# A conditioned linear layer and a mixture of experts in float32: a reordered first block, moved low parts, and a woven seam between the shared part and the experts

## The reference, cut to what matters

```python
ys = y / sqrt(512)                                        # conditioned linear layer
d  = rsqrt(einsum('bi,io->bo', ys*ys, weight*weight) + 1e-8)
x  = x + einsum('bsi,io->bso', x * ys[:, None, :], weight) * d[:, None, :]

shared = silu(x @ w1) * (x @ w3) @ w2                     # hidden size 1024
s      = sigmoid(concat([x, t_emb]) @ router_W)           # 8 experts
pick 2 of 8 by s + router_bias, gates = s / sum of the two
routed = sum over the two experts of gate * (gelu(x @ W1e) @ W2e)   # hidden size 512
x = x + (shared + routed) / 3
```

## Time and profile before

| | us |
|---|---|
| median of 3 runs (lowest, highest) | 1060.47 (1059.27, 1061.65) |
| the profiled execution | 1054.4 |
| its span, first to last instruction | 1052.6 |
| PE busy | 1021.2 (97%) |
| DVE, ACT, POOL busy | 506.2, 293.0, 331.5 |

### The profile page before, as it was taken

One profiled execution on the slowest core, in us unless ns is written; L12 is line 12 of the kernel. 1 busy time (PEld: TensorE's weight loads), 2 busy tenths in 40 slices (PEclk: granted clock), 3 DMA queues, 4 the chain that ended last, 5 costly groups with the idle time before them and its releaser, 6 DMA issues.

```text
span 1052.6 us, 14602 instructions
## 1 busy us (share of the span) xinstructions
PE 1021.2 (97%) x4692; PEld 836.1 (79%) x4692; DVE 506.2 (48%) x828; ACT 293.0 (28%) x461; POOL 331.5 (31%) x393
## 2 busy tenths in 40 slices
PE   6999999999999999999999998999999999999996
PEld 5888778887888888888888886788888888878874
DVE  4555456668333333333322214555655566555653
ACT  3222252332222222122211112333333233332331
POOL 2000000001214433334312401365554645545533
PEclk9999999999999999999999999999999999999999
DMA  4666688787876677876833576999778999999984
GB/s 172 200 206 217 222 281 255 259 318 248 294 239 233 221 267 253 264 268 212 290 100 90 190 202 205 239 221 231 147 147 179 226 221 231 210 215 226 228 180 80
DMA packets 133259, 228.61 MB, mean 217 GB/s; under 512 B 29041, under 2 KB 83953, under 8 KB 125105
## 3 DMA queue, kind: packets, MB, share of 16 engines
q1 hardware_dynamic: 60400, 144.06, 42.8%
q0 software_dynamic: 31328, 64.11, 26.4%
q10 hardware_dynamic: 41472, 19.68, 7.9%
HBM read 112.85 MB, written 98.38 MB: 201 GB/s over the span
## 4 chain that ended last, share of the span: by engine, by line
PE 83%; DMA 8%; DVE 4%; SPq 2%; issue 2%; ACT 1%; POOLq 0%; DVEq 0%
PE banks L530 13%; PE banks L532 12%; PE banks L531 12%; PE banks L468 8%; PE banks L469 8%; PE banks L470 8%; DMA we_d<-ehl 5%; PE banks L482 4%; PE banks L483 4%; PE banks L484 4%; PE banks L416 3%; PE banks L417 3%; PE banks L418 3%; DMA eraw<-expert_w 2%; SPq L286 1%
## 5 line engine op out<-in xcount | busy, mean ns | idle before, releaser
L468 PE MATMUL banks<-xh,w 128*128 128x512 f32 x512 | 199.6, 390 | 1.8 <-DVE xl L725 1.8
L469 PE MATMUL banks<-xl,w 128*128 128x512 f32 x512 | 199.2, 389 | 0.0
L470 PE MATMUL banks<-xh,w 128*128 128x512 f32 x512 | 199.2, 389 | 0.0
L1184 POOL DMA_INDIRECT out<-ys,slot x71 | 124.0, 1746 | 181.1 <-DVE ys L1080 89.4
L792 DVE SCALAR_TENSOR_TENSOR gm<-sil,banks 128x512 f32<-128x512 f32 x64 | 43.9, 685 | 240.7 <-ACT sil L611 234.6
L1073 DVE TENSOR_TENSOR hidtl<-hidt,hidth 128x512 fp32r<-128x512 f32 x71 | 49.1, 692 | 165.9 <-ACT hidth L685 165.2
L611 ACT ACTIVATE sil<-banks 128x512 f32<-128x512 f32 x64 | 38.2, 597 | 291.9 <-PE banks L470 291.9
L1170 POOL DMA_DIRECT2D xg<-xs_d x136 | 99.9, 1108 | 58.8 <-DVE xgt L1054 49.6
L530 PE MATMUL banks<-we,hidth 128*128 x284 | 112.2, 395 | 5.8 <-issue 5.5
L530 PE MATMUL banks<-we,xgth 128*128 x284 | 111.1, 391 | 3.4 <-issue 3.4
L468 PEld LDWEIGHTS banks<-xh,w 128*128 128x128 f32 x512 | 96.1, 188 | 22.3 <-issue 2.3
(11 more groups left out here) (163 smaller groups left out, 1512.0 us busy)
## 6 DMA issues: line engine op xcount, KB each, us to landing
we_d<-ehl SPq DMA_DIRECT2D x32, 1024.0 KB, 7.3
we<-we_d SPq DMA_DIRECT2D x48, 512.0 KB
hturn<-hid ACTq DMA_DIRECT2D x284, 64.0 KB
xg<-xs_d POOLq DMA_DIRECT2D x136, 128.0 KB
eraw<-expert_w SPq DMA_DIRECT2D x32, 512.0 KB
x1t_d<-x1t SPq DMA_DIRECT2D x8, 1024.0 KB, 8.8
xin<-x1t_d SPq DMA_DIRECT2D x8, 1024.0 KB, 8.8
x_d<-x1tok SPq DMA_DIRECT2D x32, 256.0 KB
```

What stands on the lines that cost most here:

```text
L468: pe.matmul(ps[hc % 2][:, :], w_hi, xh[:, j, c, :], start=(c == 0), stop=False)
L469: pe.matmul(ps[hc % 2][:, :], w_hi, xl[:, j, c, :], start=False, stop=False)
L470: last = pe.matmul(ps[hc % 2][:, :], w_lo, xh[:, j, c, :], start=False, stop=(c == DC - 1))
L1184: pool.indirect_dma_start(out[:, :], IO(slot[:, t, 0:1], 0), ys[:, t % RING, :], None, compute_op=ALU.add).then_inc(added[t % 2], 16)
```

## The change

1. The condition's DMA goes from the head of SP's queue to the head of POOL's; the squares `w0sq` go from POOL to DVE, behind the low parts of block 0 and ahead of those of block 1.
2. `first_linear` waits for each kind of product by itself: four matmuls high x high once `wmh` and `xh` are there, four with `wml`, four with `xl`.
3. At the end of part one `x_low` runs once behind each `x1t`.
4. In block 0 of part two the first weight piece's cast and low part go from step 0 to step 1.
5. In the last block of part two `matmul1(0)` goes in between `down(7, 6)` and `down(7, 7)`, the table is read ahead of `up(7, 7)`, and DVE's and ACT's first steps of part three go into or right behind step 6 and 7 of block 7, with `take_x(1)`, `take_x(2)`, `turn_x(2)`, `turn_x(3)` ahead of `output(7)`. `hturn` and `hidth` change places in memory, so that only `h_high_of(0)` waits for `output(7)`.
6. In every tile of part three ACT's cast `x_high_of` is that of tile `t+2` and stands between `hidden(t)` and `move_h(t)`; it waits for DVE's `turn_x(t+2)`. DVE's order stays as it was for tiles 2 to 68.
7. At the end PE does `matmul1(70)` ahead of `matmul2(66)`, ACT moves tile 70 behind `h_high_of(68)`, and DVE's `take_y` goes behind `take_h`.

```diff
-        hturn = sb("hturn", [RING, SUB, P], FP32, 160)
+        hturn = sb("hturn", [RING, SUB, P], FP32, 128)
-        hidth = sb("hidth", [2, DC, P], FP32R, 132)
+        hidth = sb("hidth", [2, DC, P], FP32R, 160)
...
-            sp.dma_start(cnd[:, :, :], condT).then_inc(cond_in, 16)
...
                 for c in range(DC):
+                    pe.wait_ge(wmh_ready, c + 1)
+                    pe.wait_ge(xh_ready, c + 1)
+                    for o in range(DC):
+                        pe.matmul(lin_ps[o][:, :], wmh[:, 0, c, o * P:(o + 1) * P], xh[:, 0, c, :], start=(c == 0), stop=False)
                     pe.wait_ge(wml_ready, c + 1)
+                    for o in range(DC):
+                        pe.matmul(lin_ps[o][:, :], wml[:, 0, c, o * P:(o + 1) * P], xh[:, 0, c, :], start=False, stop=False)
                     pe.wait_ge(xl_ready, c + 1)
                     for o in range(DC):
-                        last = part(0, o, c, 0)
+                        last = pe.matmul(lin_ps[o][:, :], wmh[:, 0, c, o * P:(o + 1) * P], xl[:, 0, c, :], start=False, stop=(c == DC - 1))
...
             pe.wait_ge(tables_done, 3)
+            look_up(0)
+            up(NBLK - 1, HC - 1, 1)
+            down(NBLK - 1, HC - 2)
             pe.wait_ge(gm_done, HC * NBLK - 1 + 2)
-            look_up(0)
+            matmul1(0)
             down(NBLK - 1, HC - 1)
             pe.wait_ge(gm_done, HC * NBLK + 2)
-            for t in range(TILES + LAG):
-                if t < TILES:
+            for t in range(1, TILES + LAG):
+                if t < TILES - 1:
                     matmul1(t)
+                if t == TILES - 2:
+                    matmul1(TILES - 1)
...
             def block_steps(n, j, turn, pieces=True):
                 for hc in range(HC):
+                    if turn is None and hc == HC - 1:
+                        x_high_of(0)
                     gate(n, hc)
...
-                piece_high(0, hc)
+                if hc == 1:
+                    piece_high(0, 0)
+                if hc:
+                    piece_high(0, hc)
...
-            x_high_of(0)
+            x_high_of(1)
             for t in range(TILES + TURN_LAG):
-                if t + 1 < TILES:
-                    if t:
-                        act.wait_ge(mm1_done, t)
-                    x_high_of(t + 1)
                 if t < TILES:
                     hidden(t)
-                    if t == 0:
-                        act.wait_ge(o_done, SUB * NBLK)
+                if t + 2 < TILES:
+                    x_high_of(t + 2)
+                if t < TILES - 1:
                     move_h(t)
+                if t == TURN_LAG:
+                    act.wait_ge(o_done, SUB * NBLK)
                 if t >= TURN_LAG:
                     h_high_of(t - TURN_LAG)
+                if t == TILES - 1:
+                    move_h(t)
...
+            for c in range(DC):
+                dve.tensor_tensor(w0sq[:, c, :], w0s[:, c, :], w0s[:, c, :], ALU.mult).then_inc(square_done, 1)
             for c in range(DC):
                 scaled_low(1, c)
...
-                    for c in (() if n == 0 else ((), (), (0,), (1, 2, 3))[o]):
+                    for c in (() if n == 0 else (o,) if n == NBLK - 1 else ((), (), (0,), (1, 2, 3))[o]):
...
+                    if n == NBLK - 1 and hc == HC - 2:
+                        turn_x(0)
+                        turn_x(1)
+                        take_x(0)
+            for t in range(2):
+                take_x(t + 1)
+                turn_x(t + 2)
...
-                if t > LAG:
+                if LAG < t < TILES - 1:
                     take_y(t - LAG - 1)
-                if t + 1 < TILES:
+                if 2 <= t < TILES - 1:
                     take_x(t + 1)
-                if t + 2 < TILES:
+                if 2 <= t < TILES - 2:
                     turn_x(t + 2)
                 if 0 <= t - TURN_LAG < TILES:
                     turn_h(t - TURN_LAG)
                     take_h(t - TURN_LAG)
+                if t >= TILES - 1:
+                    take_y(t - LAG - 1)
...
-            for c in range(DC):
-                pool.wait_ge(w0_in[c], 16)
-                pool.tensor_tensor(w0sq[:, c, :], w0s[:, c, :], w0s[:, c, :], ALU.mult).then_inc(square_done, 1)
+            pool.dma_start(cnd[:, :, :], condT).then_inc(cond_in, 16)
```

More of the change, by code:

```diff
@@ L519, in _ @@
                     down(0, HC - 1)
-            with pe.Fori(1, NBLK // 2) as h:
+            with pe.Fori(1, NBLK // 2 - 1) as h:
                 for j in range(2):
                     shared_block(2 * h + j, j)
+            shared_block(NBLK - 2, 0)
+            for hc in range(HC - 1):
+                up(NBLK - 1, hc, 1)
+                if hc:
+                    down(NBLK - 1, hc - 1)
+                else:
+                    down(NBLK - 2, HC - 1)
             def product(ps, high, low, place, m, midway):
@@ L631, in piece_high, with x_high_of @@
                     act.activation(ehl[:, j, 0], eraw[:, j, 1], ACT.Copy).then_inc(eh_ready, 1)
+            def x_high_of(t):
+                act.wait_ge(xturn_done, t + 1)
+                act.activation(xgth[:, t % 2], xgt[:, t % 2], ACT.Copy).then_inc(xgth_done, 1)
             def block_steps(n, j, turn, pieces=True):
                 for hc in range(HC):
+                    if turn is None and hc == HC - 1:
+                        x_high_of(0)
                     gate(n, hc)
@@ L659, in _ @@
             block_steps(NBLK - 1, 1, None, False)
-            def x_high_of(t):
-                act.wait_ge(xturn_done, t + 1)
-                act.activation(xgth[:, t % 2], xgt[:, t % 2], ACT.Copy).then_inc(xgth_done, 1)
             def hidden(t):
@@ L1009, in _ @@
                     choose(1)
-                piece_low(0, hc)
+                if hc == 1:
+                    piece_low(0, 0)
+                if hc:
+                    piece_low(0, hc)
             for hc in range(HC):
@@ L1039, in _ @@
                         piece_low(2 * h + j, hc)
-            for n in (NBLK - 2, NBLK - 1):
-                for hc in range(HC):
-                    block_step(n, hc, n % 2, n < NBLK - 1)
-                    if hc == 0:
-                        output(n - 1)
             def turn_x(t):
@@ L1060, in take_x @@
                 dve.tensor_tensor(xgtl[:, t % 2], xgt[:, t % 2], xgth[:, t % 2].bitcast(FP32), ALU.subtract).then_inc(xgt_done, 1)
+            for n in (NBLK - 2, NBLK - 1):
+                for hc in range(HC):
+                    block_step(n, hc, n % 2, n < NBLK - 1)
+                    if hc == 0:
+                        output(n - 1)
+                    if n == NBLK - 1 and hc == HC - 2:
[5 more added lines that the diff above has]
+                turn_x(t + 2)
             def turn_h(t):
@@ L1088, in scatter_waits @@
                 dve.tensor_scalar(wait_for[0:1, 1:TILES], same[0:1, 1:TILES], 16.0, None, ALU.mult).then_inc(waits_done, 1)
-            turn_x(0)
-            turn_x(1)
-            take_x(0)
             output(NBLK - 1)
```

## The result

The changed kernel takes **1087.15 us** (median of 6 runs, 1085.92 to 1090.38) against 1060.72 (6 runs, 1058.67 to 1065.06) for the kernel before, run beside it: a ratio of 1.0248, 95% interval 1.0224 to 1.0271. It is slower by 26 us where the prediction had it 9 us faster. It went the way of the first rival, the ring, at a price higher than the 1077.7 us given there.

The account below looks back on a forecast made before the run. TensorE bounds the kernel at 2.4 GHz, so only its idle time can be won. Terms 2.0 + 1.2 + 0.3 + 4.5 + 0 + 0.7 = 8.7 gave a median of 1051.8 us, range 1046 to 1060.

Parts of the forecast that it names:

- the first rival, the ring: Part three's tiles: DMA issues wait behind the cast, closing a 5.91 us chain per tile, +25.7, 1077.7 us; chance 0.17.
- Every tile of part three: ACT's cast of tile t+2 ahead of the DMA issues costs 0, since the issues don't wait with it.
- The 1119 us: Part three: issues also wait for the cast to end, 0.63 more a tile; chance 0.03.
- The start: First matmul 2.0 us earlier, needing only `wmh` and `xh`; condition's load from POOL and squares on DVE cost 0.
- the worse bound: At the kernel's start: the condition's load from POOL lands at 7.4, a loss of 1.3 us.
- End of part one: One low part instead of three behind the last `x1t`: part two starts 1.2 us earlier, bounds 1.0 and 1.3.
- The first piece: Part two, block 0: wait of 1.7 for `gl` goes, wait for `output` grows; gain 0.3, bounds 0 and 1.9.
- its own sign of being wrong: Start of block 2 in part two: the wait for `output` still 1.0 instead of 2 to 3 us.
- The rival that this seam keeps its 1.9: Part two's weight pieces are not rigid: 1.9 gained instead of 0.3, end 2.1 instead of 0.7, 1048.8 us; chance 0.14.
- Beginning of the experts: Seam to part three: woven first products fill PE's idle time before `matmul2(0)`; gain 4.5, bounds 3.5 and 4.7.
- The end: Last tiles: `matmul1(70)` goes forward, so the last `matmul2`s find their input; gain 0.7, bounds 0 and 2.1.

Follow-up runs that it names:

- experiment 2: Changed kernel, same ACT order, but DVE turns the x of tile t+3 instead of t+2: 1056.89 us, ratio 0.9971.
- experiment 4: Kernel before with only ACT's cast of tile t+2 put between the gelu and the move: 1094.27 us, ratio 1.0334.
- experiment 7: Kernel before with first-block products by kind, low parts behind each move and squares on DVE; condition's load stays on SP: 1053.80 us, ratio 0.9961.
- experiment 3: Changed kernel with the cast of x behind the move and `h_high`, condition's load back at the head of SP's queue: 1051.80 us, ratio 0.9931.
- experiment 1: Changed kernel with only ACT's cast of x put back behind the move and `h_high`: 1052.74 us, ratio 0.9944.
- experiment 8: Kernel before with only the first weight piece's high and low parts moved from step 0 to step 1: 1057.44 us, ratio 0.9986.
- experiment 9: Kernel before with only `h_high(t-2)` put ahead of `move_h(t)`: 1050.66 us, ratio 0.9917.
- experiment 10: Kernel before with products by kind, low parts behind each `x1t`, first piece at step 1, squares on DVE, `h_high` ahead of the move: 1046.46 us, ratio 0.9871.
- experiment 5: Changed kernel with condition's load on SP, `h_high(t-2)` ahead of `move_h(t)` and the cast of x last: 1041.79 us, ratio 0.9845.

## Why the prediction was wrong, and where it was right

**The step that failed** is the one in "Every tile of part three": "So the engine's reading goes on to the DMAs, which start when `hidden(t)` is done, as now." They don't: they start 0.01 us behind the start of the waiting cast. The reading was argued from PE's release gaps (0.06 and 0.21 us), on another engine, for matmuls, which wait in order behind one another anyway. It said that a carried wait is released sooner, which may well be, but not that a later instruction gets past it. The prediction named this as its weak point and still gave the rival 0.17. And the trace of the kernel before could have settled it. In part two a register operation, which waits for nothing, often stands right behind an activation on ACT that had to wait for its semaphore; in all 40 places where ACT had idled over 0.3 us before such an activation, the register operation starts 0.005 to 0.009 us behind the activation's start and never during the wait. What stands behind a waiting activation on ACT waits with it, and that was there to be read before the change was run. The Trainium skill ("Perfetto Trace Analysis", the parts on DVE and Act instructions and on HWDGE) draws the sequencer as free once an activation is in the wait queue; experiment 2 agrees in one half (the issue doesn't wait for the work), experiments 2 and 4 together show the other half not to hold here (it does wait for the wait).

**The rival's price** was nearly right where it was worked out. Its 5.91 a tile is 5.94 in the tile from 795.43 to 801.37. The mean is 6.07, and link by link the trace shows why: 1.87 from `take_h` to `turn_x`, 0.74 from there to the cast and 0.66 from `h_high` to `take_h` are as put in the sum; from the cast to `h_high`, which is the four issues, it is 2.80 in the mean for the 2.62 of the earlier trace rows, and up to 3.57, as in the fence above. Over 66 tiles the 0.16 a tile makes 10.6. With 3.3 less gained up to the tiles (4.2 for 7.5) and 1.3 less behind them (0.3 lost for 1.0 gained) that is 15.2 above the rival's sum for the profiled execution (1071.6, against 1086.87); 5.8 of it don't show in the median, since from the profiled execution to the median it is only 0.3 in the kernel after. What is left, 9.4, is 1087.15 - 1077.7. The 1119 us that would follow from waiting for the cast's end too is excluded by experiment 2.

**The start**: 2.0 was right for the order of the products (8.48 and 8.46 in experiments 7 and 3), wrong for the load, so that in all 0.2 was lost (10.43 to 10.65), where 2.0 was forecast. Its landing 7.4 us after the issue from POOL, at 8.7, lies beyond the worse bound, a landing at 7.4; it cost 2.2 of the start where that bound had 1.3. That bound took the row of 6.9 as the worst case and measured it from 0.5, while the issue started at 1.32. The reason for taking 0 was that the row of 6.9 had a load ahead of it; here none stood ahead on POOL's queue and the load was as slow, 6.9 and 6.8 in the traces of experiments 1 and 2. The loads of the other two queues, eight of them issued between 0.85 and 3.3, may be the cause, but they are there too when SP or ACT issues the condition and it lands in 2.2 to 4.0. Which of the two it is, POOL's issue itself or the crowd, stays open.

**End of part one**: 1.2, measured 1.21 in the stall (1.84 to 0.63). Right. In the kernel after only 0.4 is left of it at part two: the start takes 0.2, and 0.6 goes in PE's first block, which lasts 10.54 to the demodulation instead of 9.98, since some 12 matmuls run at half rate instead of 9. That 0.6 is not the change's: in the kernels of experiments 4, 8 and 9, whose start is the same as before's, this stretch takes 11.19, 9.63 and 11.03. And the term left something out. Before's stall is 2.11 from matmul to matmul, and in three of the four traces that have it (experiments 4, 8 and 9, not before's own) the clock falls behind it, with 7 or 8 matmuls at 0.43 us, some 1.4 us more; with the shorter stall, 0.91, it falls in none of ten. The stretch behind it, in experiment 8 and in before (the clock is the third number from the end):

```profile
116.00:119.00 3.00, 3.00 (x9) 2.33 (x8) 1.72 (x3) 0.00 (x0) 0.00 (x0) 0.50 0.94 251
```

```profile
116.00:119.00 3.00, 3.00 (x14) 2.45 (x14) 1.86 (x3) 0.00 (x0) 0.00 (x0) 1.00 0.91 276
```

So item 3 can be worth more than its 1.2; the one trace that the prediction was made from doesn't show this.

**The first piece**: the size holds, the place doesn't. 0.3 was forecast, with bounds 0 and 1.9; the trace of experiment 8 has 0.8 less waiting, and from part two's first matmul to that of block 3 after takes 198.6 and before 198.7. But the wait that comes back is not the one the prediction named, 2 to 3 us for `output` in block 2. That one stays at 1.1, which is its own sign of being wrong, and a new one of 1.6 comes a block earlier. That DVE falls behind was right, where it does was not. The rival that this seam keeps its 1.9 falls by the traces; the runs of experiment 8 alone (up to 3.8 us gained) wouldn't exclude it.

**Beginning of the experts**: 4.5, bounds 3.5 and 4.7. In the kernel after it gave 3.7, for the pause ahead of `matmul2(0)` was 3.16 instead of 2.3, and the clock fell behind it. With `h_high` ahead of the issues it gave 5.7 (experiments 10 and 5), beyond the bounds. The forecast had the chain right (gelu, four issues, cast, low part) and didn't ask whether the issues have to stand in it.

**The end**: 0.7 was forecast. In the order of the forecast's kernel nothing of it can be told; with `h_high` ahead of the move it costs about 1.1 by six traces (44.3 for 42.9 to 43.6), which the runs can't tell. The prediction saw that scatter 70 waits for scatter 68 and still counted the earlier products as a gain.

**What the prediction did not have**: the order of `h_high` and the move. The row that showed it, 2.6 us of "issue" ahead of `hidth`, was used as a term of a sum and not as a wait to be removed. By the medians it is worth 8.8 us alone and 9.1 on top of the rest, the second from ratios on two chips (0.9931 and 0.9845); the profiled executions of that pair, 3 and 5, are only 2.0 apart, since that of 3 is the fastest of its seven.

With item 6's place and the load on POOL undone the sum comes near: the forecast was 8.7, experiment 3 has a ratio of 0.9931 (0.9909 to 0.9954), which is 7.3 us (4.9 to 9.6). Part of that is luck: the seam gave less than its term and the end nothing, while the clock behind the stall, which is in no term, gave something back.

## What to carry to other kernels

A DMA issue behind an activation that waits is late by that wait, though not by that activation's work: beware of anything ahead of an issue that waits, through other engines, for what is queued behind that issue, and put the short step that PE waits for ahead of the issues, not behind them. Add up the ring that an order closes and set it against what the busiest engine needs: with the cast of x ahead of the issues it is 5.9 to 6.1 us, with `h_high` ahead of them 5.3, and PE needs 5.44. Look for such a question's answer in the trace first, in any place where the same engine has the same pair of instructions, as above with the register operations. Where two readings of a queue give 0 and +26 us and the new place gains nothing by itself, choose the order that is right under both. Once PE is 95% busy, look for the engine that issues rather than computes: here the tile had 2.6 us of issues on ACT ahead of a cast of 0.6.

## What the runs showed of the hardware

- ACT's DMA issue starts 0.01 us (median of 69) behind the start of a waiting activation ahead of it, and 0.03 behind the end of the gelu that it needs when the activation between them has no wait left, while that activation still runs (experiment 2). Register operations behind a waiting activation do the same (0.005 to 0.009 us behind its start, 40 places in before).
- An 8 KB load issued by POOL as the first of its queue landed 7.4, 6.9 and 6.8 us after its issue (after, experiments 1 and 2), among the loads of the start; the same load took 2.2 and 2.5 at the head of ACT's queue and 3.0 to 4.0 at the head of SP's.
- The clock behind a pause of PE, in the traces of all fourteen kernels behind 30 us (pauses from the start of one matmul to that of the next). Eight of 2.65 to 3.55 us: behind each of them, 5 to 13 matmuls 0.43 us apart, the rate of the lower level of 1.2 GHz, in place of 0.23. Eight of 2.30 to 2.58: behind three of them. Nine of 1.92 to 2.20: behind none. Left out of these nine is the stall of 2.11 us at the end of part one, which comes right behind 32 short products of the router: behind it such matmuls stand in three of four kernels. At 0.2 us each, 7 or 8 such matmuls make a pause cost some 1.5 us more than itself. That the clock follows how busy PE has just been is also what the Trainium skill says ("TensorE: Matmul & The Clock Gate", Part 1).
- The same drop stands behind 3.63 us of products with 4 columns, in eleven of fourteen kernels. No kernel without these products was run, so that they are its cause is not shown.
